# Where the value products and the other work stand within an attention step

## The reference, cut to what matters

```python
h = _modulate(_ln(x), sh_msa, sc_msa)
qkv = (h @ w_qkv + b_qkv).reshape(B, N, 3, nh, hd).transpose(2, 0, 3, 1, 4)
q, k, v = (qkv[0], qkv[1], qkv[2])
attn = jax.nn.softmax(jnp.einsum('bhqd,bhkd->bhqk', q, k) * hd ** (-0.5), axis=-1)
o = jnp.einsum('bhqk,bhkd->bhqd', attn, v).transpose(0, 2, 1, 3).reshape(B, N, C)
o = o @ w_proj + b_proj
x = x + g_msa[:, None, :] * o
```

## Time and profile before

| | us |
|---|---|
| Median of 3 runs | 2031.09 (2029.89 to 2041.32) |
| The profiled execution | 2030.6 |
| Its span, first to last instruction | 2028.9 |
| PE busy | 1829.6 (90%) |
| DVE busy | 1218.1 (60%) |
| ACT busy | 958.4 (47%) |
| Mean granted TensorE clock | 0.925 of full speed |

### The profile page before, as it was taken

One profiled execution on the slowest core, in us unless ns is written; L12 is line 12 of the kernel. 1 busy time (PEld: TensorE's weight loads), 2 busy tenths in 40 slices (PEclk: granted clock), 3 DMA queues, 4 the chain that ended last, 5 costly groups with the idle time before them and its releaser, 6 DMA issues.

```text
span 2028.9 us, 30253 instructions
## 1 busy us (share of the span) xinstructions
PE 1829.6 (90%) x10259; PEld 1196.8 (59%) x10259; DVE 1218.1 (60%) x2619; ACT 958.4 (47%) x1739; POOL 540.0 (27%) x1431
## 2 busy tenths in 40 slices
PE   5798999989999999999679999989987788989998
PEld 4452445436898989898334444448963344434697
DVE  3654777755455464645567777725546677775544
ACT  2144545555444454544155565554432556555542
POOL 0001444555666653534023233430000000000000
PEclk9578989998999999999689999969996889999899
DMA  6335211212010020200222212111003222221100
GB/s 193 107 86 139 87 58 62 69 50 76 1 44 21 0 64 1 64 1 0 95 76 80 67 53 85 35 62 51 1 1 114 67 70 76 64 78 49 48 13 36
DMA packets 69969, 118.99 MB, mean 59 GB/s; under 512 B 8144, under 2 KB 31451, under 8 KB 69780
## 3 DMA queue, kind: packets, MB, share of 16 engines
q1 hardware_dynamic: 65348, 105.00, 16.5%
q0 software_dynamic: 2064, 8.80, 1.8%
q10 hardware_dynamic: 2416, 3.42, 0.5%
HBM read 85.28 MB, written 31.73 MB: 58 GB/s over the span
## 4 chain that ended last, share of the span: by engine, by line
PE 63%; DVE 13%; DMA 8%; SPq 6%; ACT 5%; issue 4%; POOL 0%; DVEq 0%; ACTq 0%
PE ps L873 17%; PE ps L884 16%; PE ps L756 6%; PE ps L745 5%; DMA qk_rows<-qk 5%; DVE mx L1415 5%; PE ps L645 4%; PE ps L696 4%; SPq L376 3%; ACT pT L1102 2%; PE ps L732 2%; DMA qs<-nmT 2%; PE ps L652 1%; SPq L384 1%; PE ps L685 1%
## 5 line engine op out<-in xcount | busy, mean ns | idle before, releaser
L1415 DVE TENSOR_REDUCE mx<-ps 128x1 f32<-128x512 f32 x768 | 485.4, 683 | 126.6 <-PE ps L732 118.5
L1102 ACT ACTIVATE pT<-ps 128x512 f32<-128x512 f32 x768 | 416.1, 593 | 292.8 <-PE ps L745 287.2
L732 PE MATMUL ps<-ks,qs 54*128 54x512 f32 x768 | 338.2, 523 | 68.5 <-DMA ks<-qk_rows 47.0
L745 PE MATMUL ps<-qs,ks 56*128 56x512 f32 x768 | 321.3, 495 | 56.9 <-ACT pT L1102 35.6
L1361 DVE TENSOR_TENSOR gl<-gf,gh 128x512 fp32r<-128x512 f32 x216 | 149.9, 695 | 273.2 <-ACT gh L1033 271.1
L1032 ACT ACTIVATE gf<-ps,cols 128x512 f32<-128x512 f32 x216 | 148.8, 689 | 339.7 <-PE ps L873 339.2
L745 PEld LDWEIGHTS ps<-qs,ks 56*128 56x128 f32 x768 | 129.0, 198 | 270.7 <-ACT pT L1102 145.1
L884 PE MATMUL ps<-w2h,gh 128*128 128x288 f32 x864 | 255.7, 296 | 1.6 <-DVE tmpx L1448 1.3
L884 PE MATMUL ps<-w2h,gl 128*128 128x288 f32 x864 | 254.7, 295 | 0.0
L884 PE MATMUL ps<-w2l,gh 128*128 128x288 f32 x864 | 254.1, 294 | 0.0
L756 PE MATMUL ps<-pT,vaug 128*32 128x512 f32 x1536 | 227.9, 664 | 0.0
(11 more groups left out here) (185 smaller groups left out, 2805.7 us busy)
## 6 DMA issues: line engine op xcount, KB each, us to landing
qk_rows<-qk SPq DMA_DIRECT2D x96, 252.0 KB
qs<-qk_rows SPq DMA_DIRECT2D x96, 144.0 KB
ks<-qk_rows SPq DMA_DIRECT2D x96, 144.0 KB
w1raw<-in_w SPq DMA_DIRECT2D x18, 576.0 KB, 4.1
w2raw<-in_w SPq DMA_DIRECT2D x18, 432.0 KB, 4.9
qs<-qk_rows SPq DMA_DIRECT2D x96, 72.0 KB
ks<-qk_rows SPq DMA_DIRECT2D x96, 72.0 KB
wfc<-in_w_skew POOLq DMA_DIRECT2D x4, 1152.0 KB, 9.8
```

The costliest lines, as they stand in the source:

```text
L732: ins = mm(bank(MAX_BANKS[v % 3]), qs[at:at + KMAX, buf, h // 2, qt * P:(qt + 1) * P], ks[at:at + KMAX, buf, h // 2, :], start=True, stop= ...
L745: ins = mm(bank(2 + i % 2), ks[at:at + KROW, b % 2, h // 2, kt * P:(kt + 1) * P], qs[at:at + KROW, b % 2, h // 2, :], start=True, stop=Tru ...
L1102: A(pT[:, kt % 2 * HG + i, :], bank(2 + i % 2), ACT.Exp, scale=SCALE).then_inc(S["exp_done"], 1)
L1415: V.tensor_reduce(mx[:, g % NG, qt, column(i):column(i) + 1], bank(MAX_BANKS[(NU * g + qt * HG + i - first) % 3]), AX.X, ALU.max).then_inc ...
```

## The change

`walk` gets a new order. Before, a step was: tiles 0 and 1, A, tiles 2 and 3, B, value products, C. Now it is: tile 0, A, tile 1, value products, tile 2, B, tile 3, C. ACT's copy at `sums_out` moves with the value products. On DVE alone, the kinds P and T1 at place A (`low_part` and `split_h1`) come after tile 1 instead of directly after tile 0; the rest of A comes after tile 0. No instruction is added or removed, and the table of the other work is the same.

```diff
-def walk(tile, others, pv):
+def walk(tile, others, pv, behind=()):
 
     for g in range(NG):
         for kt in range(TT):
-            tile(g, kt, (0, 1))
-            others(g, kt, "A")
-            tile(g, kt, (2, 3))
-            others(g, kt, "B")
+            tile(g, kt, (0,))
+            others(g, kt, "A", lambda kind: kind not in behind)
+            tile(g, kt, (1,))
+            others(g, kt, "A", lambda kind: kind in behind)
             pv(g, kt)
-            others(g, kt, "C")
+            tile(g, kt, (2,))
+            others(g, kt, "B", lambda kind: True)
+            tile(g, kt, (3,))
+            others(g, kt, "C", lambda kind: True)
...
-                def others(g, kt, place):
+                def others(g, kt, place, now):
                     for kind, arg in other_work(g, kt, place, l, b):
+                        if not now(kind):
+                            continue
...
-                    walk(tiles, others, lambda g, kt: None)
+                    walk(tiles, others, lambda g, kt: None, ("P", "T1"))
```

## The result

The change made the kernel slower: 2083.72 us median of 4 runs (2072.28 to 2105.7) against 2031.51 (2029.89 to 2041.32), ratio 1.022 with a 95% interval of 1.0157 to 1.0283. The forecast was 2020, range 2001 to 2037: wrong in sign, and the result lies outside the range. The profiled execution took 2077.25 us, its span 2075.5, 46.6 more than before.

A forecast was written before the change was run, and what follows sets the result against it. No engine alone bounds it: the limit changes hands five times between DVE, ACT, PE and transfers, and only handovers move. Six middle items -7.2, three first -1.5, three last -2.1: -10.8 us, from 2030.6 to 2019.8, forecast 2020, range 2001 to 2037.

The forecast's parts named there:

- Change of tiling: PE, throughout: 201 more changes of matmul kind at 0.1 us each, taken as 0 with +20 us as other end.
- Rival A: Mode changes count in full wherever PE is the limit, about half of the item: 2030 to 2040 us; chance 0.16.
- Costs I put at nothing: Value products' new place, ACT's later `sums_out` and HH in POOL's chain, all taken as adding no time.
- The handovers: All instructions stay, so only handovers between engines move; their gains over all batch items sum to -10.8 us.
- Part 1: End of group 0, middle item: first turn -1.45 us, one more exponential before P0 +0.5; net -0.95.
- part 2: P0 and P1, middle item: P1's bank wait goes, -0.3 us; tile 1 comes behind P0, +0.3; net 0.
- part 3: Start of second DVE stretch, middle item: three reduces before LN2a instead of two, projection ends 0.34 earlier; net +0.35 us.
- Part 5: Group 3, middle item: P3 one tile earlier, second store some 0.25 us later after P3, transfers behind unchanged; net -0.4.
- C: Theory from the experiments, not the prediction: tiles parted by sparse other work keep PE at 1.2 GHz, wait or not.

The follow-up runs named there:

- e11: Kernel before plus one small product in each of the 192 steps, placed between tiles 2 and 3 so the pair is parted; 2058.17 us, ratio 1.0116.
- e12: Kernel before plus the same small product in each of the 192 steps, placed ahead of tile 0, parting no pair; 2045.03 us, ratio 1.0031.
- e2: Kernel before, old order, only DVE's low part of P and split of T1 one tile later; 2061.18 us, ratio 1.0112.
- e1: Changed kernel, but DVE's low part and split back at place A directly after tile 0; 2071.5 us, ratio 1.0162.
- e7: Changed order in blocks 1 and 2 alone, the old order in block 0; 2053.65 us, ratio 1.0078.
- e6: Changed order in block 0 alone, the old order in the other two blocks; 2075.06 us, ratio 1.017.
- e3: Kernel before with only the value products moved up, ahead of tiles 2 and 3, pairs kept; 2042.01 us, ratio 1.0031.
- e4: Kernel before with pairs parted (tile 0, A, tiles 1 and 2, B, value products, tile 3, C), nothing late on DVE; 2055.16 us, ratio 1.0096.
- e8: Changed kernel, but with the old order in group 2 of block 0; 2070.97 us, ratio 1.0147.
- e9: Kernel before with value products ahead of tiles 2 and 3 in each block's last batch item only, pairs whole; 2029.86 us, ratio 0.9962.
- e13: Kernel before with the changed order only in group 2 of items 1 and 2 of block 0, 8 of 192 steps; 2049.96 us, ratio 1.0075.
- e5: Changed kernel with four whole-array products added ahead of each of the 20 matrix exponential steps in block 0; 2088.13 us, ratio 1.0241.

## Why the prediction was wrong, point by point

**"Change of tiling", taken at 0: the step that failed first.** I had the number (201 more changes of kind, 0.1 us each, +20) and set it aside because "a tile behind a tile costs 0.34 as well, no less than a turn behind a tile (0.33)". Both figures are of a pair: each tile has another one beside it. No row shows what follows a single tile, and I took the second tile of a pair for one. In the changed kernel it's 0.43 to 0.44, and e11 against e12 gives 0.19 us for a pair parted. The Trainium skill's page "TensorEngine Tiling (Array Packing)", section "Key Properties", states that changing the tiling mode drains TensorE. The 0.19 us of a parted pair agrees with a price for the change, though no run shows that it is a drain. Rival A's reason was right, and its reach, "about half of the item", somewhat high (13 of 36 us). Its time, 2040, was still 44 us short of the median.

**"Costs I put at nothing".** I wrote that HH stays "two tiles and value products from the last one as before", and looked at POOL for the danger. I counted the late low part as "one tile later". But the rest of place A stands between as well: in block 0 LN2e and a step of the matrix exponential. The rule I should have used is to write out DVE's queue from the product to its low part, in every block, and to ask who waits for that bank. It costs 7.9 us of waiting instead of 1.7. In e2, where nothing else changed, the late part cost 14 us at equal clock; in the new order it cost 6 (after against e1).

**The clock wasn't a term at all.** I used it to read the earlier trace rows and then kept it as it was. The three runs of after that the ratio uses averaged 362 us at 1.2 GHz, the 46 of before 304. At 0.29 that is 17 us. The other 26 us of the loss are there at equal clock: 6 for the late low part (after against e1) and 20 for the new order without it (e1 against before).

These 20 are the size of the term that I had set to 0, and that is in part chance. By e11 only some 7 of the +20 would reach the end, and the forecast's gains come off. In blocks 1 and 2 the changes of kind would account for what is lost if nearly all of them reached the end (10 us in e7, for some 130 changes of 0.1). In block 0 they can't: 22 us in e6, for some 70 changes. The late part is in these 22, and so may be some clock: groups 2 of items 1 and 2 took 21.5 us longer, with some 47 us more at 1.2 GHz (14 at 0.29) and 5.3 us more of HH waiting. What the rest of block 0's loss is stays open.

**The handovers held, as far as they were seen.** I take item 1 of block 2 after (it starts at 1694.56), beside item 2 of before, which starts at 1732.30 (before, item 1 took 84.9 us and item 2 85.2). Timelines of PE and DVE, after:

```profile
1717.86 0.63 PE L688 MATMUL ps<-ident,xn 128*128 128x128 f32 x4 [0.81 <-DVE xn L1288]
...
1723.95 0.49 PE L648 MATMUL ps<-hTh,wqh 128*126 128x512 f32 x1 [1.05 <-ACT hTraw L1082]
...
1728.11 0.47 PE L648 MATMUL ps<-hTh,wqh 128*126 128x512 f32 x1
...
1763.25 0.50 PE L648 MATMUL ps<-hTh,wqh 128*126 128x512 f32 x1
...
1779.10 0.49 PE L748 MATMUL ps<-qs,ks 56*128 56x512 f32 x1 [1.47 <-DMA qs<-nmT]
```
```profile
1740.20 0.81 DVE L1270 BATCH_NORM_STATS2 stats<-xres 128x6 f32<-128x288 f32 x2
```
```profile
1765.96 1.84 SPq L362 DMA_DIRECT2D qk_rows<-qk  x2
1772.25 1.45 SPq L379 DMA_DIRECT2D qs<-qk_rows  x4
```

| from the item's start | before | after | change | forecast |
|---|---|---|---|---|
| first T1 | 24.57 | 23.30 | -1.27 | -1.45 |
| P0 | 30.37 | 29.39 | -0.98 | -0.95 |
| LN2a | 46.19 | 45.64 | -0.55 | -0.6 |
| P3 | 70.16 | 68.69 | -1.47 | -1.4 (-1.2, and 15.2 instead of 15.0 behind it) |
| next item | 85.19 | 84.54 | -0.65 | -1.2 |

Part 1's T1 and P0, part 2's vanished wait of P1 (no bracket at 1728.11) and part 3's LN2a are right to 0.2 us. Part 5 is where the item missed: P3 to the next score tile took 15.85 us and not 15.2. The store's issue ends 4.55 us after P3 begins (4.33 before), the loads are issued 9.00 after it (8.32 before, where the row is 1810.78). Item 2 after has T1, P0 and LN2a at the same places to 0.01 us, but P3 only at 71.37 and took 87.2 us, 2.0 more than before, with 7 us more at 1.2 GHz. So parts 1 to 3 were a fair account of both items, and the way to P3 only of item 1. They were the small end of the sum: -10.8 us hoped for, against a loss of 43 from what had been set at 0 or not thought of.

**What stays open.** What starts a long stretch at 1.2 GHz. In group 2 of items 1 and 2 of block 0, nine kernels have an order that leaves at least one pair of tiles whole (before, e2, e3, e4, e7, e8, e9, e11, e12): none had a stretch over 13.7 us in these groups. Of the five that part both pairs there, four (after, e1, e6, e13) had one of 23.9 us or more, and e5, with added work, 17.1. That ties the long stretches to the parted tiles (C), but parted tiles aren't enough either: item 1 had only 6.8 us in e1 and 10.2 in e13. A wait alone isn't enough (e2), and a long one isn't needed (e1), yet all four stretches of 27.3 us (after and e6) came with waits of HH of 2.4 or 4.6 us. The Trainium skill's page "TensorE: Matmul & The Clock Gate", section "HAM oscillation — how this bites in real kernels", puts a fall of the clock down to waits of PE; e2's stretches agree with it, the 23.9 us in e1, behind waits of 1.00 and 0.20 us, don't. Freeing HH from P2's bank wasn't tried.

## What to carry to other kernels

Keep matmuls of one tile shape together on TensorE; price each parting by the distance of starts around a tile that really stands alone, and if the trace has none, keep the mode change in the sum. When an engine's dependent step moves "one tile later", write out everything that its queue has in between, in each variant of the loop, and look for who waits for its buffer. Treat the granted clock as a term with its own range, and compare orders at equal clock where effects of 1% matter.

## What the runs showed that I had not expected

- PE busy for 27.30 of 27.30 us with the granted clock at 0.50 throughout: a busy PE is no proof that the clock comes back. A single tile there costs 0.72 us to the next work (0.43 at 2.4 GHz), a pair at 1.2 GHz in before 0.59 + 0.56.
- Eight steps of 192 in another order cost 0.75% (e13).
- Two executions of one kernel differ by up to 20 us; the clock goes with much of it (0.29 us for each us at 1.2 GHz).
